# Second 16-head attention: the relative bias enters the score bank by an fp32 identity matmul, and VectorE takes one maximum of 512 columns a group

## The reference

```
qkv = x @ w_qkv.T                               # reshaped to B=4, N=128, 3, H=16, D=8
scores = einsum('bhqd,bhkd->bhqk', q, k) * scale
scores = scores + compute_bias(N, N, rel_bias_table)    # (1, 16, 128, 128), from 32 buckets
attn = softmax(scores, axis=-1)
out = einsum('bhqk,bhkd->bhqd', attn, v)
out = out.transpose(0, 2, 1, 3).reshape(B, N, C) @ w_proj.T + b_proj
```

## Time and profile before

| | |
|---|---|
| three runs | 281.3, 279.96, 281.42 us; median 281.3 |
| profiled execution, first to last instruction (span) | 278.8 us, mean granted clock 0.907 |
| PE busy | 209.7 us (75%) |
| DVE busy | 205.7 us (74%) |
| ACT busy | 151.6 us (54%) |
| POOL busy | 74.6 us (27%) |
| the second attention | from 211.0 to some 253 us of the span |

### The profile page before, as it was taken

How to read it: one execution, slowest core, us unless ns; L and a number is a source line. 1 busy time by engine, 2 the same in 40 slices (tenths; PEclk the granted TensorE clock), 3 DMA queues, 4 the chain that set the end, 5 groups by cost and what they waited for, 6 DMA issues and landing times.

```text
span 278.8 us, 4790 instructions
## 1 busy us (share of the span) xinstructions
PE 209.7 (75%) x1557; PEld 141.2 (51%) x1559; DVE 205.7 (74%) x585; ACT 151.6 (54%) x510; POOL 74.6 (27%) x73
## 2 busy tenths in 40 slices
PE   6896988898786977777762577999996699973313
PEld 4475877676752322222131354777785688851102
DVE  6358648873069999999957975767767499985675
ACT  4357659643685555555317773245336689853420
POOL 5013000049305777777794010000001000001000
PEclk9688999999979799999996899999999899997555
DMA  7999700068830000000000005000000000000001
GB/s 225 429 393 414 317 2 2 0 74 93 94 45 0 1 0 1 0 0 0 2 1 0 1 0 150 2 0 2 0 1 0 4 1 2 0 4 0 4 0 38
DMA packets 6745, 16.06 MB, mean 58 GB/s; under 512 B 320, under 2 KB 5056, under 8 KB 5696
## 3 DMA queue, kind: packets, MB, share of 16 engines
q1 hardware_dynamic: 6720, 15.75, 19.7%
HBM read 13.39 MB, written 2.35 MB: 56 GB/s over the span
## 4 chain that ended last, share of the span: by engine, by line
PE 38%; DVE 24%; POOL 13%; issue 12%; ACT 9%; DMA 2%; POOLq 0%; SPq 0%; another core or an unknown queue 0%; DVEq 0%; ACTq 0%
PE bank L1076 31%; POOL region L392 13%; ACT probs L477 3%; PE bank L1416 3%; DVE region L775 2%; DVE region L758 2%; DMA ctx_T_sb<-ctx_T 2%; PE bank L1189 2%; DVE neg_max L753 1%; DVE xn L685 1%; DVE stats L680 1%; PE bank L1093 1%; DVE ext L1040 1%; DVE ext L1041 1%; DVE v_heads L698 1%
## 5 line engine op out<-in xcount | busy, mean ns | idle before, releaser
L1076 PE MATMUL bank<-region,early_sb 128*128 128x512 f32 x64 | 36.8, 661 | 11.8 <-POOL region L392 11.6
L392 POOL TENSOR_TENSOR region<-region 128x512 f32<-128x512 f32 x32 | 40.5, 1268 | 14.5 <-DVE region L900 14.5
L900 DVE TENSOR_TENSOR_SCAN region<-region,bank 128x512 f32<-128x512 f32 x32 | 38.7, 1211 | 0.0
L1076 PE MATMUL bank<-k_groups,region 128*128 128x128 f32 x256 | 35.7, 285 | 1.2 <-ACT k_groups L459 1.2
L1076 PEld LDWEIGHTS bank<-k_groups,region 128*128 128x128 f32 x256 | 32.2, 198 | 3.2 <-ACT k_groups L459 1.8
L361 POOL TENSOR_TENSOR xb<-x,rows_sb 128x512 f32<-128x512 f32 x3 | 3.8, 1261 | 101.0 <-DVE x L790 43.2
L477 ACT ACTIVATE probs<-bank,neg_max 128x128 f32<-128x128 f32 x64 | 22.6, 367 | 12.9 <-DVE neg_max L753 12.5
L1076 PE MATMUL bank<-ctx_T_sb,region 128*32 128x128 f32 (+1 forms) x288 | 26.8, 345 | 3.4 <-DMA ctx_T_sb<-ctx_T 2.2
L477 ACT ACTIVATE probs<-region,neg_max 128x128 f32<-128x128 f32 x64 | 24.9, 390 | 5.7 <-DVE neg_max L758 5.5
L1076 PEld LDWEIGHTS bank<-region,early_sb 128*128 128x128 f32 x64 | 10.1, 195 | 33.2 <-POOL region L392 32.6
L775 DVE COPY region<-bank 128x512 f32<-128x512 f32 x32 | 21.8, 682 | 5.6 <-PE bank L1189 5.6
(11 more groups left out here) (198 smaller groups left out, 410.1 us busy)
## 6 DMA issues: line engine op xcount, KB each, us to landing
ctx_sb<-ctx SPq DMA_DIRECT2D x4, 1024.0 KB, 24.5
ctx_T_sb<-ctx_T SPq DMA_DIRECT2D x3, 1024.0 KB, 10.5
late_sb<-late SPq DMA_DIRECT2D x1, 2416.0 KB, 18.4
bias_scratch<-bias_vec SPq DMA_DIRECT2D x1, 2040.0 KB, 24.7
ctx_T_sb<-ctx_T SPq DMA_DIRECT2D x2, 512.0 KB, 6.2
region<-bias_scratch SPq DMA_DIRECT2D x1, 1024.0 KB, 5.7
early_sb<-early SPq DMA_DIRECT2D x1, 512.0 KB, 3.7
region<-taps SPq DMA_DIRECT2D x1, 512.0 KB, 18.9
```

Of the source, the lines that this page charges most:

```text
L392: done(pool.tensor_tensor(read[:, k % 3, :], state[:, k % 3, :], c_sb[:, n % 2, :], ALU.mult), "read")
L900: done(dve.tensor_tensor_scan(state[:, k % 3, :], decay[:, k % NDA, :], bank[3 + k % 3][:, :], 0.0, ALU.mult, ALU.add), "state")
L1076: return pe.matmul(dst, lhsT, rhs, start=start, stop=stop)
```

## The change

The relative bias is no longer added by DVE. PE first multiplies the identity by the group's 512 bias columns (4 heads by 128 keys) in fp32 into the score bank, and the four score matmuls then accumulate onto it. DVE takes one negated maximum over the bank's 512 columns, four heads in one instruction, in both attentions. ACT reads the bank in both. The bank is therefore free only after the exponentials, and PE waits for `probs` in both. The wait for the bias transfer moves from DVE to PE. The tile `neg_biased` and the constant `HIGHEST` go.

```diff
@@ ACT, attention(ph)
-                        src = bank[t % 3][:, :].rearrange("p (h k) -> p h k", h=HG) if ph == 0 else neg_biased[:, t % 3]
+                        src = bank[t % 3][:, :].rearrange("p (h k) -> p h k", h=HG)
                         for j in range(HG):
                             h = HG * g + j
                             ins = act.activation(probs[:, w % 4, j, :], src[:, j, :], ACT.Exp,
-                                                 bias=neg_max[:, w % 4, j:j + 1], scale=1.0 if ph == 0 else -1.0,
+                                                 bias=neg_max[:, w % 4, j:j + 1],
                                                  accum_out=row_sum[:, v % 2, h:h + 1])
@@ DVE, attention(ph)
-                        if ph == 0:
-                            if w >= 4:
-                                dve.wait_ge(S["probs"], w - 3)
-                            done(dve.tensor_reduce(neg_max[:, w % 4, :], src, AX, ALU.max, negate=True), "neg_max")
-                        else:
-                            dve.wait_ge(S["bias_in"], 16)
-                            dve.wait_ge(S["probs"], w - 2)
-                            for j in range(HG):
-                                ins = dve.tensor_tensor_reduce(neg_biased[:, t % 3, j, :], src[:, j, :],
-                                                               rel_bias[:, HG * g + j, :], -1.0, HIGHEST,
-                                                               ALU.add, ALU.min, neg_max[:, w % 4, j:j + 1])
-                            done(ins, "neg_max")
+                        if w >= 4:
+                            dve.wait_ge(S["probs"], w - 3)
+                        done(dve.tensor_reduce(neg_max[:, w % 4, :], src, AX, ALU.max, negate=True), "neg_max")
@@ PE, attention(ph)
-                            pe.wait_ge(S["probs" if ph == 0 else "neg_max"], ph * 16 + t - 2)
+                            pe.wait_ge(S["probs"], ph * 16 + t - 2)
+                        if ph == 1:
+                            pe.wait_ge(S["bias_in"], 16)
+                            mm(bank[t % 3][:, :], ident, rel_bias[:, HG * g:HG * g + HG, :].rearrange("p h k -> p (h k)"),
+                               True, False)
                         for j in range(HG):
                             ins = mm(bank[t % 3][:, j * P:j * P + P],
-                                     q_heads[:, j, b * P:b * P + P], k_groups[:, g, b * P:b * P + P])
+                                     q_heads[:, j, b * P:b * P + P], k_groups[:, g, b * P:b * P + P],
+                                     ph == 0, ph == 0 or j == HG - 1)
                         done(ins, "scores")
```

More of the change, by code:

```diff
@@ L40 @@
 REGION = 15104
-HIGHEST = 3.4e38
 ROUND = 12582912.0
@@ L238, in two_layers @@
         hq_T = turn("swiglu", [NB, IC, P], BF16)
-        neg_biased = turn("self", [3, HG, P])
         c_gate = sb("c_gate", [P, NB])
```

## The result

| | before | after |
|---|---|---|
| median | 280.95 us (4 runs) | 287.34 us (285.95 to 288.49, 4 runs) |
| ratio, 95% interval | | 1.0228 [1.0188, 1.0268] |
| span of the profiled execution | 278.8 us | 286.7 us (its own time 288.49 us) |

The forecast was 288.0 us and 2.4% slower.

A forecast was written before the change was run, and what follows sets the result against it. PE's queue was taken to bound the second attention. Its new timetable, with 0.86 us more a group less the air and a start costing nothing, put the end +6.7 us later: 281.3 + 6.7 = 288.0 us, range 285.2 to 290.3.

The forecast's parts named there:

- PE's queue leads, with 0.32 us of air a round: Second attention, full rounds of four groups: PE limits, with 0.32 us idle of 7.70, 0.43 at the most.
- 0.86 us a group: PE time of the fp32 identity matmul before each of 16 groups' scores; bounds 0 to 1.72, in all 13.8 us.
- Exchange of DVE and ACT work worth nothing: Second attention: DVE's 3.7 us saving worth 0 while PE leads; of ACT's 2.7 us only the start uses some.
- The bank's longer hold costs nothing: Score bank held until exponentials read it: ring some 4.0 us against 6.6 of PE work, so no wait.
- The timetable: PE's new start times by group number t in the second attention: t=9 at 234.1, round 10.8, t=15 at 249.6.
- The end hangs on the last exponentials: End of second attention: last exponentials end at 253.6, +6.7 us; values and spread +5.9, so the later holds.
- The clock stays up at the start: Between 219 and 224, with PE's gaps filled, full clock expected; 1.5 us lost before, so the start costs nothing.
- Nothing behind is touched.: Work after the second attention's end stays as it was; the span only shifts, from 278.8 to 285.5.
- The sum: PE's whole new timetable added up: +6.7 us on the median, 288.0 us, 2.4% slower; chance 0.60.

The follow-up runs named there:

- e1: The changed kernel with the identity matmuls left out, so the relative bias is not added at all: 277.31 us, 0.9887 of the kernel before.
- e5: The changed kernel with each group's maximum in the second attention taken twice, once into a spare tile: 288.32 us, 1.0285 of the kernel before.
- e2: The kernel before with 16 identity matmuls added in front of the scores, their result overwritten, nothing else changed: 287.97 us, 1.0293 of the kernel before.
- e3: The kernel before with PE waiting for the exponentials, not the maximum, before rewriting a score bank in the second attention: 280.03 us, 1.0009.
- e4: The kernel before with throw-away matmuls, 6 and 18, in PE's two gaps at the start of the second attention: 279.58 us, 0.9990.
- e8: The changed kernel with throw-away matmuls in steps 16 to 18, at the end of the second attention: 287.63 us, 1.0296 of the kernel before.
- e10: The changed kernel with the bias rounded to bf16 and one bf16 identity matmul a group instead of fp32: 279.74 us, 0.9944 of the kernel before.

## Why the prediction was right, point by point

- **PE's queue leads, with 0.32 us of air a round.** Right. Without the bias matmul a round is 7.35 us of PE (e1); the reading by start times gave 7.38. The Trainium skill, "Perfetto Trace Analysis", section "Identifying the Most-Contended Engine", would judge by the share of peak arithmetic and by weight loads; these are 8.28 of 10.70 us in the changed kernel's round while PE has not a gap in it, and adding to VectorE's work did not move the round (e5). Start times of successive PE work told it, in both kernels.
- **0.86 us a group.** Right: 0.87 by start times, (10.70 - 7.35) / 4 = 0.84 as the price in a round. The 131 ns a pass of the Trainium skill, "TensorE: Matmul & The Clock Gate", section "Back-to-back issue gap", would have given an estimated 0.52; a bf16 pass took 0.218 here.
- **Exchange of DVE and ACT work worth nothing.** Only beside the identity matmuls, and there 1.07 us (e2 against the change), most of it counted in the start. Alone it is worth 2.8 us in the stage (e1): the largest thing that I read too small. The profiled stage goes from 46.78 to 54.20 us by -2.8 for the exchange (before to e1), +9.3 for the matmuls (e1 to the change, at the last values, with what the clock at the start gives back already taken off) and +0.9 for the clock in the tail.
- **The bank's longer hold costs nothing.** Right (e3).
- **The timetable.** t=5 was put 12.1 us after the stage's beginning and came at 11.94; t=9 at 23.1, came at 22.77; the round 10.8, was 10.70. Queries and keys of the last item took 0.45 us, not 0.64.
- **The end hangs on the last exponentials.** Wrong in what it hangs on. I put the exponentials at +6.7 and the values before the last transposes at +5.9 and took the later. The exponentials came at +6.35 and those values at +6.52, and PE's order shows that the values held the end. What I had left out of +5.9 is PE's 0.69 us of waiting for `x`, behind the last group's maximum and copy. That +6.52 is near the forecast +6.7 is partly luck.
- **The clock stays up at the start.** Right. Filling the gaps by other means holds it too (e4). I priced it at 1.5 us; 1.05 is what comes through to the first values.
- **"Nothing behind is touched."** Wrong in the profiled execution: the clock fell 2 us before the last projection, and the tail took 8.42 us where the kernel before took 7.52; with the clock up it is 7.52 again (e8). Whether the change brings this is not shown. The clock fell early in e2 too, and between the last values and the projection in e3 and e4, which have no identity matmul, while in e5, which has all sixteen, it stayed up.
- **The sum.** The profiled span is 7.9 us longer: +6.52 up to the last values, +0.90 in the tail, and +0.47 before the stage, which has nothing to do with the change. The forecast was +6.7, and the medians of the runs say +6.4. The mechanism and the slope are what the experiments bear out; an agreement of 0.7 us between 288.0 and 287.34 is closer than four executions that lie 2.5 us apart can show.

## What to carry to other kernels

Before work is moved to an engine, find how much air that engine has in one round of the pipeline, by start-to-start times and not by busy shares; here three engines were within 8% of each other, and only one had no room for 0.86 us more in each group. Price the moved work in the new engine's own passes: an fp32 identity matmul of 512 columns is as dear as four bf16 ones, and with one bf16 pass the loss of 2.3% was gone (0.9944 of the kernel before, and 1.0003 with fillers). A relief on an engine that does not lead can still be worth something when it is made alone; test the two halves of an exchange apart.

## What the runs showed of the hardware that I had not expected

- The granted clock can fall in the tail of a stage whose PE was full until 5 us before (250 to 254: PE busy 3.31 of 4 us; clock 0.50 from 258), and with sixteen throw-away matmuls in waiting time it was 1.00 up to 260. When it falls differs between kernels whose tails are the same: from the last values to the rounding they took 7.5, 7.8 or 8.4 to 8.6 us. The 0.9 us gained in the stage does not show in the times of whole executions.
- The first bf16 pass a group costs 0.68 us a round, the second 0.87. The traces of e1 and e10 place the difference. In the group after the values the pass costs 0.13 us (0.99 from the group's start to its transposes in e1, 230.49 to 231.48; 1.12 in e10, 228.75 to 229.87), and in the one after the projection 0.14 (1.19 with the projection in e1, 1.33 in e10); in the other two it costs 0.21. So most of the 0.10 that the scores pay in the earlier trace rows for a change of operands is gone: with the identity matmul in front they take 0.89 us in every group.
